# Spreading an expert's down product over the next expert's gate and up products, and an earlier ScalarE copy

## What is computed

```python
logits = x @ router_w
scores = jax.nn.sigmoid(logits)            # 32 experts, 8 groups; the best 4 groups, in them the best 8 experts
...
gate = jax.lax.ragged_dot(xs, w_gate, group_sizes)        # 512 -> 256, for each routed expert
up = jax.lax.ragged_dot(xs, w_up, group_sizes)            # 512 -> 256
down = jax.lax.ragged_dot(jax.nn.silu(gate) * up, w_down, group_sizes)   # 256 -> 512
routed = (down[unsort].reshape(T, K, H) * tkw[..., None]).sum(axis=1)
shared = jax.nn.silu(x @ sw_gate) * (x @ sw_up) @ sw_down
x = x + routed + shared
```

## Time and profile before

| | |
|---|---|
| median of 3 runs | 532.67 us (532.51 to 533.3) |
| the profiled execution, its own time | 532.38 us |
| span of that execution in the trace | 530.3 us |
| TensorE busy | 520.7 us, 98% of the span |
| VectorE busy | 389.1 us, 73% |
| ScalarE busy | 304.3 us, 57% |
| the loop over experts, of the span | about 260 to 516 us |

### The profile page before, as it was taken

The page is one execution under the profiler, slowest core; times in us unless marked ns, Lnnn a source line. Parts: engine busy times, 40 slices in busy tenths (PEclk is TensorE's granted clock), DMA queues, the critical chain, the costliest instruction groups (busy, mean ns, idle before and its releaser), DMA issues.

```text
span 530.3 us, 9657 instructions
## 1 busy us (share of the span) xinstructions
PE 520.7 (98%) x3454; PEld 469.0 (88%) x3454; DVE 389.1 (73%) x616; ACT 304.3 (57%) x470; POOL 29.4 (6%) x48
## 2 busy tenths in 40 slices
PE   9999999999989999989999999999999999999997
PEld 7988888888669989879989999999999999999997
DVE  6777555557788988776987777768677776767675
ACT  5665587753476776637546465554646465554631
POOL 1000000000632131010000000000000000000000
PEclk9999999999999999999999999999999999999999
DMA  8775624455412232516355646464554646455521
GB/s 286 289 231 175 209 99 155 162 159 157 127 35 78 86 136 90 199 41 237 121 183 173 203 157 222 143 225 163 193 189 167 204 161 223 146 215 171 185 71 40
DMA packets 19459, 86.24 MB, mean 163 GB/s; under 512 B 2160, under 2 KB 2416, under 8 KB 19312
## 3 DMA queue, kind: packets, MB, share of 16 engines
q1 hardware_dynamic: 19440, 85.99, 47.9%
HBM read 85.46 MB, written 0.52 MB: 162 GB/s over the span
## 4 chain that ended last, share of the span: by engine, by line
PE 92%; DVE 5%; ACT 2%; issue 1%; POOL 0%; ACTq 0%; DVEq 0%; POOLq 0%
PE bank L936 33%; PE bank L429 16%; PE bank L433 16%; PE bank L432 16%; PE bank L437 2%; PE bank L501 1%; PE bank L438 1%; PE bank L439 1%; PE bank L573 1%; DVE w_lo L282 1%; PE bank L715 1%; PE bank L735 1%; PE bank L696 1%; ACT operands L305 1%; PE bank L455 1%
## 5 line engine op out<-in xcount | busy, mean ns | idle before, releaser
L277 ACT CAST w_hi<-raw 128x768 fp32r<-128x768 f32 (+3 forms) x158 | 158.9, 1040 | 96.6 <-PE bank L936 82.8
L282 DVE TENSOR_TENSOR w_lo<-raw,w_hi 128x1280 fp32r<-128x1280 f32 (+3 forms) x156 | 182.7, 1213 | 13.5 <-ACT w_hi L277 11.4
L429 PE MATMUL bank<-w_hi,operands 128*128 128x512 f32 (+1 forms) x322 | 126.1, 392 | 1.2 <-DVE operands L330 1.0
L433 PE MATMUL bank<-w_hi,operands 128*128 128x512 f32 (+1 forms) x322 | 124.0, 385 | 0.0
L432 PE MATMUL bank<-w_lo,operands 128*128 128x512 f32 (+1 forms) x322 | 123.8, 385 | 0.0
L936 PE MATMUL bank<-xt_hi,w_lo 128*128 128x256 f32 x512 | 108.6, 283 | 0.0
L936 PE MATMUL bank<-xt_hi,w_hi 128*128 128x256 f32 x512 | 108.4, 283 | 0.0
L936 PE MATMUL bank<-xt_lo,w_hi 128*128 128x256 f32 x512 | 108.3, 283 | 0.0
L936 PEld LDWEIGHTS bank<-xt_hi,w_hi 128*128 128x128 f32 x512 | 83.7, 190 | 2.6
L936 PEld LDWEIGHTS bank<-xt_hi,w_lo 128*128 128x128 f32 x512 | 81.7, 190 | 0.0
L936 PEld LDWEIGHTS bank<-xt_lo,w_hi 128*128 128x128 f32 x512 | 81.7, 190 | 0.0
(11 more groups left out here) (182 smaller groups left out, 565.4 us busy)
## 6 DMA issues: line engine op xcount, KB each, us to landing
raw<-w_exp_dram SPq DMA_DIRECT2D x34, 896.0 KB, 4.7
raw<-w_exp_dram SPq DMA_DIRECT2D x34, 640.0 KB, 5.6
raw<-ctx_t_dram SPq DMA_DIRECT2D x16, 512.0 KB, 4.6
raw<-ctx_n_dram SPq DMA_DIRECT2D x16, 512.0 KB, 4.1
raw<-w_mla_dram SPq DMA_DIRECT2D x8, 512.0 KB, 3.6
raw<-w_mla_dram SPq DMA_DIRECT2D x8, 448.0 KB, 3.9
raw<-wq_dram SPq DMA_DIRECT2D x4, 256.0 KB, 5.4
raw<-wk_dram SPq DMA_DIRECT2D x2, 512.0 KB, 7.3
```

The source lines that it names most:

```text
L277: act.copy(w_hi[:, t.slot, at:at + n], raw[:, t.slot, at:at + n]).then_inc(hi_split[k], 1)
L282: eng.tensor_tensor(w_lo[:, t.slot, at:at + n], raw[:, t.slot, at:at + n], w_hi[:, t.slot, at:at + n].bitcast(F32), ALU.subtract) \
L429: ins = pe.matmul(o, a[0], b[0], start=start, stop=False)
L433: return pe.matmul(o, a[1], b[0], start=False, stop=stop)
```

## The change

In the loop and for gate_up(33), `down` is not called behind `gate_up` any more. Its twelve matmuls are issued singly by a new function, `down_piece`, from within the gate_up of the next expert: one after each pair of gate and up matmuls in chunks 1 and 2 of the second half (pieces 0 to 5), four within the last chunk (6 to 9), and two behind the last up matmul (10 and 11). Its waits (for the hidden rows, the down weights and the result banks) stand at pieces 0 and 6. The first 30 of the 48 gate and up matmuls are as before. Experts 0, 1 and 33 keep their down products as they were. On ScalarE the copy to `h_hi` moves ahead of the cast of part 0.

```diff
-            def gate_up(j, s, told=None):
+            def gate_up(j, s, told=None, mixed=False):
...
                         if m == 1 and c == NC - 1:
                             for u in range(2):
-                                for a, x in products:
+                                for k, (a, x) in enumerate(products):
                                     ins = gate_or_up(u, m, c, a, x)
                                     if u == 1 and a is w_lo:
                                         ins.then_inc(used[0], 1)
-                                ins.then_inc(bank_full[b + u], 1)
+                                    if k == 2:
+                                        ins.then_inc(bank_full[b + u], 1)
+                                    if mixed and 3 * u + k < 4:
+                                        down_piece(j, s - 1, 6 + 3 * u + k)
...
                                 gate_or_up(1, m, c, a, x)
+                                if mixed and m == 1 and c > 0:
+                                    down_piece(j, s - 1, 3 * c - 3 + k)
+                for i in range(10, 12 if mixed else 10):
+                    down_piece(j, s - 1, i, used[2] if i == 10 else None)
+
+            def down_piece(j, s, i, told=None):
+
+                h, m, k = i // 6, i // 3 % 2, i % 3
+                t = Tile(j, T_E + s)
+                b = 4 + 2 * (s % 2) + h
+                if i == 0:
+                    pe.wait_ge(ev_lo, j * 2 + (V_H + s))
+                    ready(t, 1)
+                if m == k == 0:
+                    pe.wait_ge(res_done, j * 4 + (2 * s + h + 1))
+                at = slice(m * T + h * P, m * T + h * P + P)
+                a, w = ((h_hi, w_hi), (h_hi, w_lo), (h_lo, w_hi))[k]
+                ins = pe.matmul(bank[b][:, :], a[:, s % 2, at], w[:, t.slot, OFF[1] + m * 512:OFF[1] + m * 512 + 512],
+                                start=m == k == 0, stop=m == 1 and k == 2)
...
             with pe.Fori(1, NE // 2 - 1) as j:
-                gate_up(j, 1, told=used[1])
-                down(j, 0, told=used[2])
-                gate_up(j, 2, told=used[1])
-                down(j, 1, told=used[2])
-            gate_up(0, NE - 1, told=used[1])
-            down(0, NE - 2, told=used[2])
+                gate_up(j, 1, told=used[1], mixed=True)
+                gate_up(j, 2, told=used[1], mixed=True)
+            gate_up(0, NE - 1, told=used[1], mixed=True)
...
                 if ahead >= 1:
                     split_hi(act, Tile(j, T_E + s + 1), 1, E_SIZES)
-                if ahead >= 2:
-                    split_hi(act, Tile(j, T_E + s + 2), 0, E_SIZES)
                 act.wait_ge(h_ready, j * 2 + (s - 1))
                 act.copy(h_hi[:, s % 2, :], h_row[:, s % 2, :]).then_inc(ev_hi, 1)
                 if ahead >= 2:
+                    split_hi(act, Tile(j, T_E + s + 2), 0, E_SIZES)
                     split_hi(act, Tile(j, T_E + s + 2), 2, E_SIZES)
```

More of the change, by code:

```diff
@@ L938, in gate_or_up @@
                                      stop=c == NC - 1 and x is xt_lo)
+                products = ((w_hi, xt_hi), (w_lo, xt_hi), (w_hi, xt_lo))
                 for m in range(2):
@@ L943, in gate_up @@
                             ready(t, 2 * c)
-                        products = ((w_hi, xt_hi), (w_lo, xt_hi), (w_hi, xt_lo))
                         if m == 1 and c == NC - 1:
                             for u in range(2):
-                                for a, x in products:
+                                for k, (a, x) in enumerate(products):
                                     ins = gate_or_up(u, m, c, a, x)
@@ L958, in gate_up @@
                                 gate_or_up(1, m, c, a, x)
+                                if mixed and m == 1 and c > 0:
[15 more added lines that the diff above has]
+                                start=m == k == 0, stop=m == 1 and k == 2)
+                if told is not None:
+                    ins.then_inc(told, 1)
+                if m == 1 and k == 2:
+                    ins.then_inc(bank_full[b], 1)
             def down(j, s, told=None):
```

## The result

The changed kernel takes 537.1 us (median of 6 runs, 535.51 to 538.23) against 532.83 us for the kernel before (6 runs, 532.51 to 533.3) on the same chip. The ratio is 1.0074, with a 95% interval of 1.0064 to 1.0085: it is slower by 4.3 us. Forecast were 535.7 and a range of 531.0 to 540.0.

| run | us | mean granted clock |
|---|---|---|
| two runs | 535.51, 535.65 | 0.999 |
| the profiled one | 536.52 | 0.997 |
| three runs | 537.67, 538.21, 538.23 | 0.994 |

A forecast was written before the change was run, and what follows sets the result against it. TensorE, busy 98% of the span, was taken to bound the kernel through its count of matmuls times their spacing. Terms -1.2 + 0 + 2.2 + 2.0 = +3.0 us gave 535.7 us, range 531.0 to 540.0.

The forecast's parts named there:

- term one: Mixed loop, experts 2 to 32: narrow matmuls behind wide ones save a little spacing; -1.2 us, between -3.1 and 0.
- rival of half the excess: Mixed loop: half of 0.43 us excess per expert goes, -6.6 us, time 530.3; shorter spacing in general had chance 0.20.
- term two: Loop: hidden rows still arrive before down piece 0, so no added wait; 0 us, with a margin of 0.25 us.
- term three: Start, expert 2's late hidden rows: 18 matmuls that covered the wait now come behind it; +2.2 us (2.0 to 2.3).
- term four: End: down_last waits for expert 33's hidden rows, which come later after the mixed gate_up(33); +2.0 us (1.8 to 2.3).
- third rival: New waits at start and end: the clock falls; at half after the first wait, 1.3 us more, 537; chance 0.04.
- My sign for it: Profile of the changed kernel: a clock row below 1.00 near 266 us would show the third rival is right.
- second rival: Loop: hidden rows late in every step; at 0.3 us for each of 31 experts, +9 us, 545; chance 0.10.

The follow-up runs named there:

- e3_both: The changed kernel with both ends as before the change, experts 3 to 31 still mixed; 531.4 us, ratio 0.9972 to the kernel before.
- e1_head: The changed kernel, but gate_up(3) runs whole with down(2) behind it, everything later mixed; 534.55 us, ratio 1.0024 to the kernel before.
- e5_no_swap: e3_both with ScalarE's old order, the copy of the rows behind the cast of part 0; 538.61 us, ratio 1.011 to the kernel before.
- e2_tail: The changed kernel, but gate_up(33) runs whole with down(32) behind it; 535.51 us, ratio 1.0041 to the kernel before.

## Why the forecast was right, point by point

**The sum was right in sign and near in size, partly because two errors met.** Forecast were +3.0 us, of which -1.2 in the loop, +2.2 at the start and +2.0 at the end. Measured without a fall of the clock: -1.45, +1.86, +1.88, and 0.11 for the first matmul behind the second wait, in all +2.4 us, so 535.2, and the two runs with 0.999 lie at 535.5 and 535.65. So the terms were 0.6 us too high, and the clock, put at nothing, makes most of the other 1.9 us to 537.1. That the two errors have opposite signs is luck. One sum of the forecast is wrong: the low ends of the terms, -3.1 + 2.0 + 1.8, make +0.7, so the low end of the time is 533.4 and not 533.6; nothing else rests on it.

**The spacing, term one:** -1.2 forecast with ends 0 and -3.1; -1.45 measured over 29 distances of the changed kernel (the two mixed gate_ups at the ends save 0.05 each as well), and 1.34 in e3_both. The one pair of 0.23 us against 0.24 pointed the right way, but with rows rounded to 0.01 us the size was partly luck. The rival of half the excess needed 0.2 us per step; there are 0.05. The reason that I gave against it, that wide ones in a row are no leaner, holds: the wide ones hardly changed (0.229 in the mean before and after). The formula that the Trainium skill gives for a matmul alone (TensorE: Matmul & The Clock Gate, section Back-to-back issue gap), 0.109 and 0.216, isn't reached here by either width (0.113 and 0.229).

**The wait in the loop, term two:** 0 forecast, 0 measured, no wait between the two ends. The margin was 0.25 us by my count of 30 matmuls. It is larger. VectorE's remainder ends 3.14 us into the step, as the row of expert 32 had it (3.13), a matmul can follow 0.22 later at 3.36, and piece 0 stands at 3.84: 0.48 us. I misread the place of the piece by one pair. The latest step, the one in which expert 6's rows are made, has the remainder at 3.47, and even that leaves 0.15.

**The start, term three:** the cause is as described, and TensorE went on 0.22 us after the remainder, as forecast. The size was off by the same pair: 16 matmuls come behind the wait and not 18, 16 x 0.120 = 1.92 and not 2.16; measured 1.86, in which the mixed gate_up(3) is itself 0.05 shorter. e1_head took the wait away.

**The end, term four:** 2.04 forecast, 1.88 measured. The links are the ones forecast: the copy starts 0.03 us behind the product, the remainder 0.03 behind the copy. The product came 0.06 later after the last up matmul than I had it, the first matmul of down_last followed the remainder in 0.05 us (527.49 to 527.54) instead of 0.22, and the mixed gate_up(33) is itself 0.05 shorter: 2.04 + 0.06 - 0.17 - 0.05 = 1.88.

**The clock, third rival:** given a chance of 0.04, because the clock was still full in the last 3.3 us of the kernel before. That was the step that failed. It came at the end in the profiled execution, and by the clocks of the runs at one or both waits in at least four of six. I priced a fall at 1.3 us; it cost 1.2 at the end, where TensorE's work runs out (1.29 less the 0.11 of the first matmul behind the wait), and 1.6 at the start. My sign for it, a clock below 1.00 near 266 us, didn't even come in the profiled execution, whose fall is at 529. What I should have asked was what the rows can say of a wait of 2 us at all. The waits in the kernel before are 1.25 us at most, and after its last matmul nothing is left to run slowly. The rows were silent and I read them as a no. The range held because it had been drawn wide enough for the clock (537) and for rows that are late by 0.1 us per step, though I gave the first 0.04.

**Late rows, second rival:** did not come, but e5_no_swap shows that it was the right danger: with the old order of ScalarE each step waits 0.24 us and the kernel is 7 us slower than e3_both.

## What to carry to other kernels

A block of work that hides a chain of other engines is missed where it is moved away, and that can cost once at each end of a loop even when the loop itself has room: ask of every moved block what it covered in the first and in the last turn, and leave those two as they were (531.4 us here, against 537.1). A wait of some 2 us on TensorE can cost more than its length, as the clock may fall behind it (1.2 to 1.6 us here); where it can't be avoided, work that nobody needs was cheaper here than standing still. And a mix of narrow and wide matmuls is worth a little, 0.005 us net for each narrow one that gets a single wide one ahead of it.

## What the runs showed of the hardware that I had not expected

- After TensorE had stood still for 1.77 us (end) or 2.19 us (start), the granted clock went from 2.4 to 1.2 GHz 1.5 us (end) or 0.9 us (start) after it had begun to work again, and in e2_tail it stayed there for 3.4 us though TensorE was busy. It does so in some executions of a kernel and not in others: five of eleven have a mean clock of 0.997 in e1_head, and five of six in e2_tail. With 14 or 16 matmuls put into the wait it did so in none of 23.
- The first matmul of 512 columns behind a wait, also behind one of 0.2 us, takes 0.32 to 0.34 us to the next one instead of 0.23.
- A matmul of 256 columns takes 0.120 us behind another of its kind, 0.113 behind one of 512 columns, and 0.113 when it loads 64 columns instead of 128 and writes half the rows. One of 512 columns takes 0.226 to 0.233 in the mean, whatever its neighbours.
